# A graph network's three layers on one core: one more slot of distance in the attention, probabilities turned by DMA instead of by TensorE

## The reference, cut

```
h = relu(layernorm(x))                                   # no scale or shift
for l in range(3):
    scores = si[:, :, None] + sj[:, None, :] + attn_b[l] # si = h @ attn_w[l, :d], sj = h @ attn_w[l, d:]
    scores = leaky_relu(scores, 0.2), -inf where neither adjacency nor the diagonal
    attn   = softmax(scores)
    agg    = einsum('bij,bjd->bid', attn, h)
    h1     = layernorm(h + agg) * g1[l] + beta1[l]
    ff     = gelu(h1 @ W1[l] + b1[l]) @ W2[l] + b2[l]    # 256 -> 1024 -> 256
    h      = layernorm(h1 + ff) * g2[l] + beta2[l]
out = x + h
```

## Time and profile before

| | |
|---|---|
| time, median of 3 runs | 2631.7 us (2631.31 to 2631.83) |
| the profiled execution | 2632.32 us |
| its span, first to last instruction | 2630.5 us |
| TensorE busy | 2283.2 us, 87% |
| weight loads | 1555.4 us, 59% |
| VectorE busy | 1775.0 us, 67% |
| ScalarE busy | 1887.8 us, 72% |
| GpSimd busy | 1904.6 us, 72% |
| mean granted TensorE clock | 0.993 of full speed |
| moved by DMA | 121.12 MB, mean 46 GB/s |

### The profile page before, as it was taken

How to read it: one execution, slowest core, us unless ns; L and a number is a source line. 1 busy time by engine, 2 the same in 40 slices (tenths; PEclk the granted TensorE clock), 3 DMA queues, 4 the chain that set the end, 5 groups by cost and what they waited for, 6 DMA issues and landing times.

```text
span 2630.5 us, 46306 instructions
## 1 busy us (share of the span) xinstructions
PE 2283.2 (87%) x15840; PEld 1555.4 (59%) x15840; DVE 1775.0 (67%) x5890; ACT 1887.8 (72%) x3498; POOL 1904.6 (72%) x1639
## 2 busy tenths in 40 slices
PE   2889999998888999998888999999888889999997
PEld 1566666665555666665555666666555566666665
DVE  5676666666776666766767676666677676666664
ACT  3777777767767777777677777776776777777774
POOL 2477777677787767777777777777778777767787
PEclk9899999999999999999999999999999999999999
DMA  5221111112232010112223111110223211011222
GB/s 158 73 57 47 23 25 17 25 33 67 75 101 49 17 25 17 25 21 53 73 77 77 41 25 21 21 25 17 57 73 101 53 17 25 17 25 17 41 55 74
DMA packets 280170, 121.12 MB, mean 46 GB/s; under 512 B 209792, under 2 KB 278400, under 8 KB 279936
## 3 DMA queue, kind: packets, MB, share of 16 engines
q1 hardware_dynamic: 279936, 118.15, 19.3%
HBM read 51.01 MB, written 16.78 MB: 26 GB/s over the span
## 4 chain that ended last, share of the span: by engine, by line
POOL 33%; ACT 31%; DVE 19%; issue 9%; PE 6%; DMA 1%; SPq 0%; POOLq 0%; DVEq 0%
POOL rstd L787 7%; ACT norm L494 6%; POOL X L833 6%; POOL X L831 6%; POOL norm L817 6%; POOL X_lo L809 5%; ACT probs L519 5%; ACT L484 5%; ACT L519 5%; ACT p_hid L484 4%; ACT g_hi L489 4%; DVE g_lo L577 4%; DVE scores L639 4%; DVE row_top L645 2%; DVE bn L584 2%
## 5 line engine op out<-in xcount | busy, mean ns | idle before, releaser
L577 DVE TENSOR_TENSOR g_lo<-p_hid,g_hi 128x512 f16<-128x512 f32 x768 | 527.8, 687 | 677.9 <-ACT g_hi L489 673.7
L401 PE MATMUL p_pair<-w_hi,g_hi 128*128 128x256 f16 x3072 | 837.8, 273 | 0.0
L401 PE MATMUL p_pair<-w_lo,g_hi 128*128 128x256 f16 x3072 | 837.6, 273 | 0.0
L401 PE MATMUL p_pair<-w_hi,g_lo 128*128 128x256 f16 x3072 | 837.4, 273 | 0.0
L484 ACT ACTIVATE p_hid<-p_hid,b_eff 128x512 f32<-128x512 f32 x768 | 504.5, 657 | 217.9 <-PE p_hid L387 216.7
L387 PE MATMUL p_hid<-hT_hi,w_hi 128*128 128x512 f16 x1536 | 458.7, 380 | 178.2 <-DVE g_lo L577 178.0
L494 ACT ACTIVATE norm<-res,shift,rstd 128x256 f32<-128x256 f32 x384 | 199.2, 589 | 409.5 <-POOL shift L789 409.5
L489 ACT ACTIVATE g_hi<-p_hid 128x512 f16<-128x512 f32 x768 | 458.5, 597 | 24.4
L387 PE MATMUL p_hid<-hT_lo,w_hi 128*128 128x512 f16 x1536 | 458.4, 380 | 0.2 <-DMA hT_lo<-h_lo 0.2
L387 PE MATMUL p_hid<-hT_hi,w_lo 128*128 128x512 f16 x1536 | 458.6, 380 | 0.0
L805 POOL TENSOR_TENSOR h_lo<-norm,h_hi 128x1024 f16<-128x1024 f32 x96 | 204.8, 2133 | 344.6 <-ACT h_hi L539 344.6
(11 more groups left out here) (67 smaller groups left out, 3662.1 us busy)
## 6 DMA issues: line engine op xcount, KB each, us to landing
x_in<-in_x SPq DMA_DIRECT2D x32, 512.0 KB, 3.8
w_f<-in_x SPq DMA_DIRECT2D x32, 512.0 KB, 5.7
out<-w_f SPq DMA_DIRECT2D x32, 512.0 KB, 5.0
adj_in<-in_adj SPq DMA_DIRECT2D x32, 256.0 KB, 4.4
w_f<-in_L_gnn_W SPq DMA_DIRECT2D x6, 1024.0 KB, 6.9
hT_hi<-h_hi SPq DMA_TRANSPOSE x96, 3.1
hT_lo<-h_lo SPq DMA_TRANSPOSE x96, 3.1
attn_rows<-in_L_gnn_attn_w SPq DMA_DIRECT2D x1, 768.0 KB, 6.6
```

The costliest lines, as they stand in the source:

```text
L401: mm = pe.matmul(ff_banks(s)[:, t, :], g[i][:, nodes], w[l][:, c, :], start=(c == 0 and t % 2 == 0 and n == 0), stop=(c == C - 1 and n == ...
L577: dve.tensor_tensor(g_lo[i][:], p_hid[k][:], g_hi[i][:], ALU.subtract).then_inc(g_lo_ready, 1)
```

## The change

Four things change.

1. Probabilities are rounded first and turned afterwards. ScalarE rounds `probs` to `p_hi` (`high_probs`), VectorE takes `p_lo = probs - p_hi`, both in SBUF; SP turns each with one DMA transpose of [128, 512] float16 into pT_hi and pT_lo. The four transposes on TensorE and the PSUM buffer for them are gone.
2. The attention is stretched by one slot. Dot products, s_j, scores and exponentials are made for an item one slot earlier than before (`s+3` and `s+4` in place of `s+2` and `s+3`); aggregation, residual and norm stay where they were to within a step (the aggregation moves from step 0 of the next slot to step 6). Input statistics and the input norm, and the loads of x, move by a slot as well; there is one slot more at the start.
3. Within the slot: the exponentials go from step 4 to 5, the scores from 3 to 4 (behind the g_lo of that step), `feed_statistics` to step 3, `low_probs` and `row_sums` to step 1, `dot_products` to step 5.
4. On GpSimd `inverse_deviation` for the attention norm stands first in the slot.

The ring stays at eight groups.

```diff
-FIRST_SLOT = -5
+FIRST_SLOT = -6
-FOLD_AT = {0: 0, 2: 1, 4: 2}
+FOLD_AT = {0: 0, 3: 1, 5: 2}
...
         def sj_bank(s):
-            return agg_banks(s)[:, 0:2, :].rearrange("p a (u n) -> p (a u) n", n=N)
+            return p_pair[s % 2][:, 0:2, :].rearrange("p a (u n) -> p (a u) n", n=N)
...
+            def turn_probs_lo(r, s):
+                sp.wait_ge(p_lo_ready, total(r, s, 1, 1))
+                if later(r, s):
+                    sp.wait_ge(agg_ready, total(r, s - 1, 1, 1))
+                sp.dma_start_transpose(pT_lo[:], p_lo[:].rearrange("p t n -> p (t n)")).then_inc(pT_lo_ready, 16)
...
+                if is_item(r, s + 2):
+                    turn_probs_lo(r, s + 2)
                 if is_item(r, s + 1):
                     turn_h(r, s + 1)
+                if is_item(r, s + 3):
+                    turn_probs_hi(r, s + 3)
...
             def spread_sj(r, s):
-                if later(r, s, 3):
-                    pe.wait_ge(res2_ready, total(r, s - 3, 2, 2))
+                if later(r, s, 4):
+                    pe.wait_ge(res2_ready, total(r, s - 4, 2, 2))
...
             def aggregate(r, s):
-                pe.wait_ge(pT_lo_ready, total(r, s, 1, 1))
+                pe.wait_ge(pT_hi_ready, total(r, s, 16, 16))
+                pe.wait_ge(pT_lo_ready, total(r, s, 16, 16))
                 pe.wait_ge(X_lo_ready, total(r, s, 1, 1))
+                if is_item(r, s + 1):
+                    pe.wait_ge(score_steps, total(r, s + 1, 5, 4))
...
-                    if c == 7 and is_item(r, s + 2):
-                        transpose_probs(r, s + 2)
...
-                    if c == 3 and is_item(r, s + 2):
-                        spread_sj(r, s + 2)
-                    if c == 0 and is_item(r, s + 1):
-                        aggregate(r, s + 1)
+                    if c == 3 and is_item(r, s + 3):
+                        spread_sj(r, s + 3)
+                    if c == 6 and is_item(r, s + 2):
+                        aggregate(r, s + 2)
...
+            def high_probs(r, s):
+                act.wait_ge(probs_ready, total(r, s, 4, 4))
+                if later(r, s):
+                    act.wait_ge(pT_hi_ready, total(r, s - 1, 16, 16))
+                act.activation(p_hi[:], probs[:], ACT.Copy).then_inc(p_hi_ready, 1)
...
             def low_probs(r, s):
-                dve.wait_ge(pT_hi_ready, total(r, s, 1, 1))
...
+                dve.wait_ge(p_hi_ready, total(r, s, 1, 1))
+                if later(r, s):
+                    dve.wait_ge(pT_lo_ready, total(r, s - 1, 16, 16))
+                dve.tensor_tensor(p_lo[:], probs[:], p_hi[:], ALU.subtract).then_inc(p_lo_ready, 1)
```

More of the change, by code:

```diff
@@ L191, in gnn_kernel @@
         row_inv = sb("row_inv", [P, T])
-        pT_hi, pT_lo = sb("pT_hi", [P, TN], F16), sb("pT_lo", [P, TN], F16)
+        p_hi, p_lo = sb("p_hi", [P, T, N], F16), sb("p_lo", [P, T, N], F16)
+        pT_hi, pT_lo = sb("pT_hi", [P, T, N], F16), sb("pT_lo", [P, T, N], F16)
         X_hi, X_lo = sb("X_hi", [P, T, D], F16), sb("X_lo", [P, T, D], F16)
@@ L520, in exponentials @@
                                    accum_out=row_sum[:, t:t + 1]).then_inc(probs_ready, 1)
-            def copy_probs(r, s):
-                act.wait_ge(pT_psum, total(r, s, 1, 1))
-                act.activation(pT_hi[:].rearrange("p (t n) -> p t n", n=N), pT_bank(s), ACT.Copy).then_inc(pT_hi_ready, 1)
+            def high_probs(r, s):
[3 more added lines that the diff above has]
+                act.activation(p_hi[:], probs[:], ACT.Copy).then_inc(p_hi_ready, 1)
             def high_X(r, s):
@@ L554, in slot @@
                         high_X(r, s + 2)
-                    if c == 4 and is_item(r, s + 2):
-                        exponentials(r, s + 2)
-                    if c == 6 and is_item(r, s + 2):
-                        copy_probs(r, s + 2)
-                    if c == 7 and is_item(r, s + 4) and layer_of(s + 4) == 0:
-                        norm_input(r, s + 4)
+                    if c == 5 and is_item(r, s + 3):
+                        exponentials(r, s + 3)
+                        high_probs(r, s + 3)
+                    if c == 7 and is_item(r, s + 5) and layer_of(s + 5) == 0:
+                        norm_input(r, s + 5)
             slots(act, slot)
@@ L666, in low_probs @@
             def low_probs(r, s):
-                dve.wait_ge(pT_hi_ready, total(r, s, 1, 1))
-                dve.tensor_tensor(pT_lo[:].rearrange("p (t n) -> p t n", n=N), pT_bank(s),
-                                  pT_hi[:].rearrange("p (t n) -> p t n", n=N), ALU.subtract).then_inc(pT_lo_ready, 1)
+                dve.wait_ge(p_hi_ready, total(r, s, 1, 1))
+                if later(r, s):
+                    dve.wait_ge(pT_lo_ready, total(r, s - 1, 16, 16))
+                dve.tensor_tensor(p_lo[:], probs[:], p_hi[:], ALU.subtract).then_inc(p_lo_ready, 1)
             def feed_residual(r, s):
@@ L704, in slot @@
             def slot(r, s):
-                starts = is_item(r, s + 5) and layer_of(s + 5) == 0
-                late = isinstance(r, int) and (r, s) == (0, -4)
-                if isinstance(r, int) and (r, s) == (0, -3):
+                starts = is_item(r, s + 6) and layer_of(s + 6) == 0
+                late = isinstance(r, int) and (r, s) == (0, -5)
+                if isinstance(r, int) and (r, s) == (0, -4):
                     dve.wait_ge(attn_dma, 2 * 16)
@@ new lines, in slot @@
+                    if c == 3 and is_item(r, s - 1):
+                        feed_statistics(r, s - 1)
+                    if c == 1 and is_item(r, s + 2):
+                        low_probs(r, s + 2)
+                        row_sums(r, s + 2)
+                    if c == 3 and isinstance(r, int) and r == 0 and s + 3 in FOLD_AT:
+                        add_bias(FOLD_AT[s + 3], sj_bank(s + 3))
+                    if c == 4 and is_item(r, s + 3):
+                        add_scores(r, s + 3)
+                        row_maxima(r, s + 3)
```

60 lines of the change are left out of this document (24 added, 36 removed).

## The result

The changed kernel takes 2354.8 us (median of 4 runs, 2352.9 to 2356.0) against 2631.8 (4 runs, 2631.3 to 2632.6): ratio 0.8947, 95% interval 0.8931 to 0.8962. The forecast was 2323, so the direction, the mechanism and most of the size hold, and 32 us are missing. The profiled execution took 2355.95 us, its span 2354.2.

The account below looks back on a forecast made before the run. GpSimd's list ahead of the attention's rstd was taken to set the slots, with TensorE next. Slots of 22.8, 23.2 and 24.0 us save 335 over four rings; 2632.3 - 335 + 26 = 2323 us, range 2285 to 2445.

Parts of the forecast that it names:

- The loop, the walk: GpSimd's list delaying the attention's rstd set 25.57 us a slot; a timed walk through the changed slot gave 22.8.
- ordinary slot: A slot without layer-0 start or layer-2 end work; 25.57 us before, 22.8 forecast, counted 16 times a ring.
- two loops: In ordinary slots, TensorE's work at 22.64 us and the norm loop at 22.2; 22.8 taken because they nearly tie.
- full slots: Six slots of a ring's 24 with statistics of x and mask, forecast 24.0 us each.
- 83.7 us a ring: Gain per ring of 24 slots, 555.2 us against 638.9; 335 over four rings.
- the inputs move to SBUF, and 0.1 us either way bounds that: VectorE's p_lo subtraction stays at 0.68 us, as g_lo, though its inputs move from PSUM to SBUF.
- my 23.7 for VectorE's loop: VectorE's loop in slots with statistics of x and mask sums to 23.7 us; 24.0 was taken.
- the slip of rows: Two score rows were assigned to items 24 and 48 but belong to 25 and 49; the first ring seemed 34 us longer.
- (a): TensorE and norm loops tie and handovers add up: ordinary slots 24.0, others 25.2, total 2445 us; chance 0.20.
- (b): Load of x lands 2 us later, lengthening six slots a ring by 2: total 2371 us; chance 0.12.
- (c): The half-turn of p_lo, queued on SP, becomes the aggregation's wait: about 2760 us at a 16 us turn; chance 0.05.
- (d): The loop is merely moved, to h_lo on GpSimd or another wait: no change, near 2632 us; chance 0.03.

Follow-up runs that it names:

- e1: Kernel before with one edit, the attention norm's rstd and shift first in GpSimd's slot: 2361.0 us, ratio 0.8966.
- e6: Changed kernel with the probabilities turned by TensorE behind the spread of s_j instead of by DMA: 2344.2 us, ratio 0.8904.
- e11: Changed kernel with six extra 128x512 matmuls, result overwritten, ahead of the spread of s_j in six slots of a ring: 2349.4 us, ratio 0.8910.
- e3: Changed kernel with p_lo and the reciprocal ahead of the statistics of x on VectorE: 2335.9 us, ratio 0.8872.
- e9: Kernel of e5 with h_lo ahead of the input's rstd and the skip connection on GpSimd: 2328.4 us, ratio 0.8831.
- e5: Changed kernel with the spread of s_j behind hidden 4, a step later on TensorE: 2329.1 us, ratio 0.8840.
- e8: Changed kernel with p_lo, the reciprocal and the statistics of x behind the feed residual on VectorE: 2341.5 us, ratio 0.8886.
- e12: Kernel of e9 with the probabilities turned by TensorE as in e6: 2331.9 us, ratio 0.8847.
- e4: Changed kernel with the four transposes of the spread of s_j done twice on TensorE, same result: 2395.4 us, ratio 0.9093.

## Why the prediction was right, and where 32 us went

**The loop, the walk.** Right. In an ordinary slot of the kernel after (time 0 at 1392.57, from the aggregation at 1388.65 and 1.31 + 2.61) norm starts at 8.1 (walk 7.9 to 8.1), p_lo is written at 7.9 (8.0), X_lo ends at 15.3 (15.4), the exponentials start at 16.2 (16.2), h_lo ends at 17.4 (17.6). I added 0.2 us to the larger of two loops because they nearly tie; they don't add, and the slot is 22.59. TensorE's share is 94%, not 95: of its 134 idle us 49 lie between 200 and 2265 us, most of them the holes of the full slots, and 70 before 200.

**What the prediction did not do** is to price the move of rstd apart from the rest. It credited the loop's cut to that line, as e1 shows rightly, but let "the change" bring 83.7 us a ring as one. e1's ordinary slot could have been read from the same count: 23.1.

**The term that was mis-sized: the full slots.** I wrote 24.0 for six and 23.2 for two. Measured are 24.2 to 27.5 and 24.04; over the run they cost 38 us more than my terms. The step that failed is "the inputs move to SBUF, and 0.1 us either way bounds that", and with it the mask at 0.66. From my 23.7 for VectorE's loop the slots close: 23.7 + 0.71 (mask at 1.39) + 0.64 (p_lo at 1.32) + 1.68 (clock) = 26.7, measured 26.90; without these but with 0.47 of waiting for x 24.2, measured 24.52; in e6, mask at 2.44 and no p_lo, 23.7 + 1.78 - 0.68 = 24.8, measured 24.89. (That last sum leaves out two terms which cancel: the four transposes, 0.44 on the chain of e6's full slot, and p_hi's copy, 0.5, which is no longer in the exponentials' block.) Of these terms the clock's has an experiment of its own, e11. p_lo's is what e3 removes by order alone, and e6 with the turn as a whole. The mask's price (1.8 us in e6 and e9) is read from rows; no kernel here moves the mask away from GpSimd's passes.

The terms don't simply come off. Take the clock's away (e11) and the load of x sets the slot at 25.2; take the spread's place away (e5) and the collisions do, at 25.23. Two or three loops lie within a microsecond there, which is why e5, e9 and e11 gave less than I expected; in e3 and e8 holes of over 2.1 us stayed, and the clock fell behind most of them.

**The counting.** I took 83.7 off four times. The last ring has 23 intervals and four full ones, as no next round starts: by my own terms it gains 72, so 12 us were booked that no slot could give.

**What is given back.** I booked 26: 12 for the deeper pipeline and 14 for a start that would not follow. The last item's end took 20.1 more and the start 1.2 less: 19. The 14 rested on the slip of rows: the first 24 items took 644.4, only 5.5 over a ring, and they gained 79.6, the most of the four stretches.

The sum: 38 (full slots) + 12 (count) - 10 (ordinary slots at 22.59 instead of 22.8) - 7 (give-back) = 33 us over the 2323, measured 32.

**The rivals.** (a) did not come: the waits of ordinary slots for g_lo are 0.4 us in all; two tied loops cost nothing at the handovers. (b) came in small: the load lands in 4.3 instead of 3.8, and there are 25.6 us of waiting for it, 13 times, 21.4 of them in the first 90 us. (c) and (d) did not come: the half-turn lands in 2.4 us at the median,

```profile
DMA to landing us min/median/max: 2.4/2.4/6.0
```

and is there at 10.3 (7.9 + 2.4), where I had it at 11 to 13. The Trainium skill's figure for a 128x128 block on the crossbar (VectorE: DVE Perf Modes, The three transpose paths), 1309 ns, would by my estimate have made this 5.2; four blocks land in 2.4 and eight in 3.1, so the blocks of one transpose do not come one after the other at that price. The Trainium skill's advice (the same page, Rules for kernel authors), TensorE for a 128x128 block where PSUM will do, held here all the same: by 10.6 us in e6, for a reason that it doesn't give, by my reading the subtraction's input in PSUM. In e12 against e9 it did not, by 3.5.

## What to carry to other kernels

Read the order of the engine that the others wait for before the units that are to be saved: one line moved to the head of GpSimd's list gave 271 of 277 us, and two such moves on the old kernel beat the whole change. When an input moves from PSUM to SBUF, look at what the neighbour on the shared port does at that moment: an instruction of 0.68 us can take up to the rest of a 2.35 us pass more. And once the largest wait is gone, several loops tie; an experiment that removes one is worth the distance to the next, not its own length.

## What the runs showed of the hardware that I had not expected

- VectorE instructions with two SBUF inputs wait out a running GpSimd pass of 512 or more columns: the mask operation took 0.68, 1.39 or 2.47 us, p_lo 0.68 or 1.32, each of these long ones ending 0.54 to 0.56 us after the pass. The same subtraction with one input in PSUM never took over 0.69. GpSimd's next instruction pays too: 1.59 for 1.27.
- TensorE's granted clock fell to 0.51 for some 3.5 us after holes of only 1.9 to 3.1 us in an otherwise full engine: 43 times of 72 over thirteen traces, and after none of 316 holes of 1.0 to 1.9 us. Six matmuls more in such a hole made the kernel 5.4 us faster.
- A crossbar turn of four 128x128 blocks lands in 2.4 us, of eight in 3.1. With two more of them a slot, the load of x landed in 4.2 to 4.4 us in eight kernels, against 3.5 to 3.8 without; e4, with them, had 3.8.
